# Attention with two heads side by side in the array, and its output projection beside the last batches

## The reference, cut to what matters

```
x = x + tanh(g_xattn[0]) * L0_xattn(layernorm(x), ctx)     # the stage that is changed
x = x + tanh(g_ffn[0])   * L0_experts(layernorm(x))        # 14 routed + 2 shared
x = x + tanh(g_xattn[1]) * L1_xattn(layernorm(x), ctx)
x = x + tanh(g_ffn[1])   * L1_experts(layernorm(x))
def L0_xattn(tgt, src):                                    # 16 heads of 16 features
    q, k, v = tgt @ Wq + bq, src @ Wk + bk, src @ Wv + bv
    w = softmax(q @ k.T / sqrt(16))
    return concat_heads(w @ v) @ Wo + bo
```

## Time and profile before

| what | us |
|---|---|
| median of three runs | 966.05 |
| profiled execution | 963.44 |
| its span, first to last instruction | 961.70 |
| TensorE busy | 754.5 (78%) |
| VectorE busy | 619.2 (64%) |
| ScalarE busy | 481.3 (50%) |
| GpSimd busy | 410.3 (43%) |

### The profile page before, as it was taken

How to read it: one execution, slowest core, us unless ns; L and a number is a source line. 1 busy time by engine, 2 the same in 40 slices (tenths; PEclk the granted TensorE clock), 3 DMA queues, 4 the chain that set the end, 5 groups by cost and what they waited for, 6 DMA issues and landing times. The chain is left out here.

```text
span 961.7 us, 20435 instructions
## 1 busy us (share of the span) xinstructions
PE 754.5 (78%) x6519; PEld 573.3 (60%) x6519; DVE 619.2 (64%) x1458; ACT 481.3 (50%) x989; POOL 410.3 (43%) x437
## 2 busy tenths in 40 slices
PE   4679999999977398979888889578777548998830
PEld 2356667667656398978666656467666526665420
DVE  8567677767664669873444444377788436666766
ACT  4736565556544467652333333245655236776632
POOL 4268323233160028881000000586856716746455
PEclk9779999999999669999999999788989868999985
DMA  6447322223170238753222221378532212323233
GB/s 159 114 103 164 92 61 67 56 64 77 30 243 9 90 88 274 236 186 114 72 66 67 68 70 48 103 192 206 162 107 67 63 53 91 115 72 96 83 90 100
DMA packets 84511, 101.50 MB, mean 106 GB/s; under 512 B 16518, under 2 KB 70758, under 8 KB 84422
## 3 DMA queue, kind: packets, MB, share of 16 engines
q1 hardware_dynamic: 69526, 68.42, 25.4%
q0 software_dynamic: 12960, 30.74, 11.4%
q10 hardware_dynamic: 1936, 1.17, 0.5%
HBM read 61.03 MB, written 24.38 MB: 89 GB/s over the span
## 5 line engine op out<-in xcount | busy, mean ns | idle before, releaser
L645 DVE TENSOR_REDUCE a_mx<-ps 112x2 f32<-112x750 f32 x128 | 119.8, 936 | 45.1 <-PE ps L323 38.7
L529 ACT ACTIVATE a_Pf<-ps 125x672 f32<-125x672 f32 x128 | 89.7, 729 | 15.6 <-PE ps L271 14.6
L323 PE MATMUL ps<-a_stkK,a_stkQ 96*112 96x375 bf16 x256 | 68.2, 349 | 20.8 <-DMA a_stkK<-a_KS 10.6
L51 PE MATMUL ps<-f_w2hi,f_hh 128*128 (+1 forms) x292 | 81.3, 278 | 3.1 <-DVE f_hl L1432 3.1
L1430 DVE CAST f_hh<-ps 128x512 bf16<-128x512 f32 x41 | 28.4, 692 | 83.9 <-PE ps L1171 83.9
L51 PE MATMUL ps<-f_w2lo,f_hh 128*128 (+1 forms) x292 | 81.2, 278 | 0.0
L51 PE MATMUL ps<-f_w2hi,f_hl 128*128 (+1 forms) x292 | 81.1, 278 | 0.0
L51 PE MATMUL ps<-f_w1hi,f_xgThi 128*128 x150 | 57.9, 386 | 23.6 <-DVE f_xgTlo L1423 17.7
L1719 POOL MEMSET a_half<- 112x2 f32 x1 | 0.1, 94 | 170.3 <-POOLq L89 170.3
L546 POOL DMA_DIRECT2D a_stkK<-a_KS x96 | 51.2, 540 | 45.7 <-DVE a_KS L612 28.9
L540 POOL TENSOR_TENSOR a_ctxL<-a_ctxF,a_ctxH 128x750 bf16<-128x750 f32 x16 | 25.7, 1604 | 104.7 <-ACT a_ctxH L429 104.7
(11 more groups left out here) (403 smaller groups left out, 2367.9 us busy)
## 6 DMA issues: line engine op xcount, KB each, us to landing
a_raw<-F_w SPq DMA_DIRECT2D x22, 512.0 KB, 5.9
f_xg<-f_xd SPq DMA_DIRECT2D x75, 128.0 KB, 2.2
f_yd<-f_yo SPq DMA_DIRECT2D x75, 128.0 KB, 1.7
f_raw<-F_w SPq DMA_DIRECT2D x14, 512.0 KB, 4.1
a_ctxF<-ctxT SPq DMA_DIRECT2D x16, 375.0 KB, 3.5
a_cR<-ctx SPq DMA_DIRECT2D x16, 375.0 KB
a_cT_first<-ctxT SPq DMA_DIRECT2D x14, 375.0 KB, 4.9
f_xd<-a_zero POOLq DMA_DIRECT2D x1, 5248.0 KB, 20.0
```

The costliest lines, as they stand in the source:

```text
L51: ins = nc.tensor.matmul(out, l, r, start=first and i == 0, stop=last and i == len(steps) - 1)
L323: last = nc.tensor.matmul(psMX[:T, h, :S], stkQ[0:96, bass.ds(n.b, 1), j // JJ, j % JJ, h * T:(h + 1) * T].rearrange("p o q -> p (o q)"), ...
L529: nc.scalar.activation(Pf[:, s % PB], psST[:C, s % 2, :SC, :QW], ACT.Exp).then_inc(exp_done, 1)
L645: nc.vector.reduce_max(mx[:, n.odd, 2 * j:2 * j + 2], psMX[:T, :, :S], AX).then_inc(mx_red, 1)
```

## The change

- Each head has its own rows. Head h of a pair stands in partitions 64h to 64h + 47 (3 parts of 16 features), with the two rows for the maximum behind them. The queries are not masked; `maxima` contract over 48 rows, twice per step, `scores` over 50 rows, six matmuls of 112 columns per step instead of three of 224. The two heads of a pair write to different PSUM banks. The factor 1/4 moves into the exp.
- Key pieces are 24 a batch instead of 12, of 16 partitions instead of 32 and one run of 750 elements each: 12 from SP and 12 from POOL. SP's are cut in 6 and 6 around `place_maxima`. A placement takes four DMAs instead of two. Keys are made three batches ahead instead of two.
- Query pieces of the first four batches are shared by SP and POOL, the others issued later by ACT and POOL.
- In a step the order on PE is maxima, values, scores, keys, `turn_values`. `values` writes to a free corner of bank 0 (`psPV`), so every second `scores` waits for the copy `oT`. PE's and POOL's lists are written out; SP, ACT and DVE keep their loop over batches 3 to 10.
- `output_projection` is gone as a stage. Its first three groups run in the lists of batches 13, 14 and 15, the last one after them. The zero fill is 14 DMAs of ACT, one a batch, and POOL's bias additions stand in the lists of batches 8 to 11.

```diff
-        stkQ = sb("stkQ", [98, B, KD, JJ, QW], BF16)
-        stkK = sb("stkK", [98, 4, KD, JJ, S], BF16)
+        SIDE, KEYS, DOT = P // 2, 3 * DH, 3 * DH + 2
+        stkQ = sb("stkQ", [P, JJ, B, KD, T], BF16)
+        stkK = sb("stkK", [P, 4, JJ, KD, S], BF16)
...
-        psPV = k.ps[:, 6, 0:T]
+        psPV = k.ps[:, 0, SC * T:(SC + 1) * T]
...
-        PIECES = [(jj, a, part) for a, part in ((0, 0), (1, 1), (2, 0)) for jj in range(JJ)]
+        PIECES = [(jj, h, a, part) for a, part in ((0, 0), (1, 1), (2, 0)) for jj in range(JJ) for h in range(2)]
+        K_SP, K_POOL = PIECES[0::2], PIECES[1::2]
...
                 def place_maxima(n, half):
                     sp.wait_ge(turn_free, 2 * n.b + half + 1)
-                    for part in range(2):
-                        sp.dma_start(stkQ[96 + part:97 + part, bass.ds(n.b, 1), half].rearrange("o b j (h q) -> o (b j h) q", q=T),
-                                     cneg[:, n.odd, half, part, :]).then_inc(c_in[half][n.odd], 16)
+                    for h in range(2):
+                        for part in range(2):
+                            row = SIDE * h + KEYS + part
+                            sp.dma_start(stkQ[row:row + 1, :, bass.ds(n.b, 1), half, :].rearrange("o j b q -> o (j b) q"),
+                                         cneg[JJ * h:JJ * (h + 1), n.odd, half, part, :]).then_inc(c_in[half][n.odd], 16)
...
+                def stack_keys(w, pieces):
+                    at_least(sp, st_full, w.b * NJ - 4 * NJ)
+                    sp.wait_ge(k_free, w.b * KD + KD)
+                    for jj, h, a, part in pieces:
+                        sp.dma_start(stkK[SIDE * h + DH * a:SIDE * h + DH * (a + 1), w.slot, jj],
+                                     KS[2 * DH * jj + DH * h:2 * DH * jj + DH * (h + 1), w.odd, part]).then_inc(k_sp[w.slot], 16)
...
+                    split = 0 if len(ws) == 2 else 6
+                    for w in ws[-1:]:
+                        if split:
+                            stack_keys(w, K_SP[:split])
                     if n is not None:
                         place_maxima(n, 0)
+                    for w in ws[-1:]:
+                        stack_keys(w, K_SP[split:])
...
                     for c in range(SC):
-                        last = nc.tensor.matmul(psST[:C, j % 2, c, :QW],
-                                                stkK[:, b.slot, j // JJ, j % JJ, c * C:(c + 1) * C],
-                                                stkQ[:, bass.ds(b.b, 1), j // JJ, j % JJ, :].rearrange("p o q -> p (o q)"),
-                                                start=True, stop=True)
+                        for h in range(2):
+                            side = slice(SIDE * h, SIDE * h + DOT)
+                            last = nc.tensor.matmul(psST[:C, j % 2, h, c * T:(c + 1) * T],
+                                                    stkK[side, b.slot, j % JJ, j // JJ, c * C:(c + 1) * C],
+                                                    stkQ[side, j % JJ, bass.ds(b.b, 1), j // JJ, :].rearrange("p o q -> p (o q)"),
+                                                    start=True, stop=True)
...
+                for t in range(KD):
+                    turn_rows(LAST, t)
+                for n in range(GB * LAST, B):
+                    project_rows(n)
```

More of the change, by code:

```diff
@@ L205, in run, with task_at, product, maxima_of @@
                 some = lambda r: (at(r),) if at(r) else ()
[L206 to L215, removed]
+                emit(at(-1), at(0), at(1), some(3), some(4), some(5))
+        def task_at(ws, s):
+            if len(ws) == 2:
+                return ws[s // 4], s % 4
+            return (ws[0], s // 2) if ws and s % 2 == 0 else (None, None)
+        def product(w, i):
+            early = isinstance(w.b, int) and w.b in (1, 2) and i % 2 == 1
+            return k.ps[:, 0, :] if early else psP
+        def maxima_of(n, j):
+            early = isinstance(n.b, int) and n.b == 0 and j % 2 == 1
+            return k.ps[:, 2:4, :] if early else psMX
+        def stack_queries(eng, batches, pieces, stacked):
+            for jj, h, i, part in pieces:
+                eng.dma_start(stkQ[SIDE * h + DH * i:SIDE * h + DH * (i + 1), jj, batches],
+                              QS[2 * DH * jj + DH * h:2 * DH * jj + DH * (h + 1), part, batches]).then_inc(stacked, 16)
         with nc.Block() as block:
@@ L235, in emit @@
                         place_maxima(b, 1)
-                    for row in l:
+                    for row in l[0:1]:
                         load(row)
[L238 to L243, removed]
+                    for w in ws[1:]:
+                        stack_keys(ws[0], K_SP)
@@ L363, in _ @@
                 turn_tokens(2)
+                keys(ring(0), 1)
                 queries(1, 0)
@@ L366, in _ @@
                 turn_tokens(3)
-                keys(ring(0), 1)
                 queries(2, 0)
@@ L391, in emit @@
                             turn_maxima(b, 1)
+                        row, g = (p, 3) if s == 1 else (b, s // 2 - 1)
+                        if row is not None and s % 2 == 1:
+                            values(row, g, p.b * NJ + NJ if b is None else b.b * NJ + s)
+                        if b is not None:
+                            scores(b, s)
                         if n is not None and s == 4:
                             turn_maxima(n, 0)
-                        if w is not None and s % 2 == 0:
-                            (keys if s < 4 else vals)(w, s // 2 % 2)
@@ L396, in emit @@
-                        if b is not None:
-                            scores(b, s)
-                        row, g = (p, 3) if s == 1 else (b, s // 2 - 1)
-                        if row is not None and s % 2 == 1:
-                            values(row, g)
-                    if n is not None and isinstance(n.b, int) and n.b == GB - 1:
-                        for g in range(1, NG):
-                            pe.wait_ge(q_in[g], 3 * JJ * 16)
-                run(pe, emit)
+                        w, t = task_at(ws, s)
@@ new lines, in emit @@
+                    if n is not None and n.b in (GB - 1, Q_TURN - 1):
+                        pe.wait_ge(rest_q, 16 * (len(Q_POOL) + (0 if n.b == GB - 1 else len(Q_PIECES))))
+                        pe.wait_ge(act_q, 16 * len(Q_ACT))
+                emit(None, None, ring(0), (ring(1), ring(2)), None, None)
+                for b in range(B + 1):
+                    p, b, n, w = (ring(b + d) if 0 <= b + d < B else None for d in (-1, 0, 1, 3))
+                    emit(p, b, n, (w,) if w else (), None, None)
@@ L632, in _ @@
                 moments(3)
+                low_keys(ring(0), 1)
                 normed(3)
@@ L635, in _ @@
                 queries(1)
-                low_keys(ring(0), 1)
                 x_low(3)
@@ new lines, in emit @@
+                        if b is None and p is not None and s == 1:
+                            for r in range(3):
+                                row_moments(r)
+                run(dve, emit)
+                done = 3
+                for r in range(done, done + 6):
+                    row_moments(r)
+                for t in range(KD):
+                    rows_low(LAST, t)
+                for r in range(done + 6, GB * LAST - 1):
+                    row_moments(r)
+                for r in range(GB * LAST, B):
+                    add_rows(r)
+                    row_moments(r - 1)
@@ L754, in linker @@
+                row_moments(B - 1)
+                for r in range(B):
+                    dve.wait_ge(y_st, r + 1)
+                    nc.vector.bn_aggr(k.mv[:, r, :], stats[:, r, :]).then_inc(y_var, 1)
+                dve.wait_ge(y_var, B)
 def linker(engine, sem):
```

412 lines of the change are left out of this document (216 added, 196 removed).

## The result

The changed kernel takes **974.06 us** (median of 8 runs, 969.97 to 978.97) against 966.27 us (963.08 to 970.23) for the kernel before, run beside it. The ratio is 1.0079, with a 95% interval of 1.0056 to 1.0101. Predicted were 937.5 us with a range of 918 to 956. The forecast was wrong in sign, and so were all rivals with a price but the one that was given 0.05.

What follows compares the result with a forecast made beforehand. TensorE looked like the bound, its steps falling from 15.04 to 13.7 us a batch, with SyncE's chain next at 14.4. The last aggregate at 293.2 instead of 321.76 took 28.6 off 963.44: 934.8, plus 2.6 gives 937.5 us (918 to 956).

Steps and rivals of the forecast that it cites:

- The steps: TensorE and VectorE's eight steps a batch, two heavy: each 0.17 us shorter, 13.7 us a batch instead of 15.04.
- the ring: Light step of TensorE and VectorE around one PSUM pair: 1.64 us before, 1.5 forecast as maxima pairs start together.
- First maxima: Startup: the first maxima matmuls start at about 39 us instead of 45.48.
- SyncE's chain: Closed once a batch: scores, low keys, six pieces, four placements, landing, next scores; forecast 14.4 us (13.6 to 15.3).
- the tail: Batches 13 to 15 and output projection: last aggregate ends at 293.2 us instead of 321.76, including the earlier gains.
- the scores' 48 short matmuls: Scores as 48 matmuls of 112 columns instead of 24 of 224: taken as same cost; half to double possible.
- 11.4 + 6c = 14.4: Sum of the once-a-batch chain through SyncE in us; c = 0.50 is a key piece's 0.45 plus 0.05 between issues.
- scores to low keys: First link of the chain: 6.25 us before, +0.95 for scores ahead of keys, -0.35 for shorter steps, 6.85.
- landing: Last link of the chain: the last placement's landing, about 2.0 us, before the next batch's scores may start.
- dear-piece rival: Key pieces on SyncE at c = 0.65: 15.3 us a batch, only the ends gain, 952.6 us; chance 0.15.
- SyncE becomes the bound outright: Issues dearer, 0.75 a piece and 0.90 a placement: 17 us a batch, 974 us, slower above 16.4; chance 0.05.
- Array switching: TensorE's array drains at some ten more mode switches a batch, 0.18 us each: +1 us a batch, 951; chance 0.10.

Runs made afterwards that it cites:

- share6: Changed kernel with SyncE issuing 6 of a batch's 24 key pieces instead of 12, all behind the first placements, GpSimd 18: 934.71 us, ratio 0.9651.
- order12p2: Changed kernel, pieces still 12 and 12, SyncE's first placements ahead of new pieces and two placements merged into one DMA: 936.84 us, ratio 0.9717.
- place2: Changed kernel with the two halves' placements of the same part merged into one DMA, 4 issues a batch instead of 8: 947.74 us, ratio 0.9798.
- busy20: Changed kernel plus twenty unused matmuls of 176 columns on TensorE ahead of each batch's first scores' wait: 966.37 us, ratio 0.9983.
- split3: Changed kernel with 3 instead of 6 of SyncE's key pieces ahead of the first four placements, 9 behind: 959.68 us, ratio 0.9921.
- split9: Changed kernel with 9 instead of 6 of SyncE's key pieces ahead of the first placements, 3 behind: 1006.59 us, ratio 1.0395.

## Why the prediction was wrong

**Where it was right.** The steps: 13.7 us a batch was forecast for TensorE and VectorE alone, and with the chain out of the way share6 takes 13.79, order12p2 13.74. The maxima's two halves start together, the ring is 1.49 (1.5). First maxima 39.52 (39). Batch 12 to batch 15 in share6 takes 43.12 (41.9 predicted: 14.3 and twice 13.8), batch 15 to the end 24.41 (22.15; 23.34 in the kernel after). TensorE's longest waits are on a_stkQ<-a_cneg at the first scores, at 1.4 to 2.8 us instead of 1. SyncE's chain was named with its right members and called the thing that is late next. Neither the tail nor the scores' 48 short matmuls (six in 0.38, three in 0.45 before) brought a loss.

**The step that failed is the sum of that chain**, 11.4 + 6c = 14.4. By the batch at 230.39 its terms were off by these amounts (measured less predicted):

| term | predicted | measured | off |
|---|---|---|---|
| scores to low keys | 6.85 | 7.96 | +1.11 |
| six pieces | 3.00 | 3.73 | +0.73 |
| gaps | 0.35 | 0.25 | -0.10 |
| placements to the last issue | 2.20 | 2.34 | +0.14 |
| landing | 2.00 | 2.45 | +0.45 |
| sum | 14.40 | 16.73 | +2.33 |

- The price of a piece was taken in the middle of two rows, 0.45. The row on the same two tensors was right and the row of like shape was not; place2 shows why shape is a poor guide, since twice the runs cost nothing. The dear-piece rival covered this, and its 15.3 us a batch would have been 952.6 (its sum comes to 308.6, not 308.3, so 952.9).
- What carried the result beyond that rival was the clock. The chain had no term for what a wait does to the engine that waits. I took 1.00 from the earlier trace rows, a stretch of a kernel that hardly waits, into one that I myself predicted to wait in each batch. busy20 prices it: 1.19 us a batch. The loop feeds itself: the wait lowers the clock, the slower matmuls delay the low keys, these delay the pieces, and the next wait is longer.
- The landing was taken from key pieces as about 2.0, below even the shortest in the row named for it (2.1 to 2.7). It was 2.45 in this batch, and 1.6 to 2.7 over the eleven.
- Single issues of some 1.5 us (L264's longest is 1.698) lengthen some batches further: in the longest, of 18.78, the six pieces took 4.64. They took as long in the shortest, of 15.60, where the clock had held and the landing was 1.64; so these issues alone do not set a batch's length.

**The sums after it.** Batches 1 to 12 took 186.47 us instead of 157.8 (229.1 less 71.3): +28.7. Batch 1 starts at 76.90 instead of 71.3 (+5.6), of which the 30 pieces at 0.12 more make 3.6. Batch 12 to 13 takes 16.14 instead of 14.3 (+1.8), the two after it 28.86 instead of 27.6 (+1.3), the last 23.34 instead of 22.15 (+1.2). With +28.7 these are 38.6, all of the 38.5 us between 293.2 and 331.71.

**The rivals.** "SyncE becomes the bound outright" gave 974 and 17 us a batch with a turning point at 16.4. The numbers came true by luck, its mechanism did not: issues did not get dearer to 0.75 (0.589 in the median, a placement 0.596 and not 0.90), SyncE idles in the batch shown from 235.98, the end of its load, to 238.38, and split3 and split9 show that its sum does not set the time. The turning point was nearly right: with this kernel's own start and end it is (321.76 - 76.90 - 68.34) / 11 = 16.05, where 68.34 is from batch 12's first scores to the last aggregate's end. Array switching: no run shows a loss by it. share6's 13.79 holds the switches as well, and next to the 13.7 forecast without them that leaves little room for the 1 us of that rival. This is argued from a forecast and not shown: no run changed the switches alone.

## What to carry to other kernels

When work on a queue is doubled, write down for each thing on it when its reader needs it, and put what is needed next ahead of what has a batch to spare, above all when a lookahead has just been lengthened. Close each chain that repeats once a period and add it up at the lower clock as well: here a wait of 1.4 to 2.8 us on TensorE in each period cost another 1.2 behind it. For a DMA's issue cost take the row with the same kind of source and destination rather than the one with the same shape, and merge issues before moving them: share6 (6 and 18 pieces) and order12p2 (12 and 12, placements merged) both beat the kernel before by about 3%.

## What the runs showed of the hardware that was not expected

- An SBUF-to-SBUF issue on SyncE took 0.588 to 0.600 us in the median for 16 partitions in one run, 32 in two, 4 runs into one partition, or 8 into two; only the old placement, 8 rows of 112 into one partition, took 0.698. The 0.32 of the earlier trace rows was for a read from DRAM, and the context's load, also from DRAM, took 0.392. What makes the difference was not tried. On GpSimd the piece of 16 partitions took 0.484 to issue, the old one of 32 took 0.536.
- The granted clock did not fall behind every wait. Behind 1.63 us at 198.00 and 1.81 at 163.94 it stayed at 1.00; behind 1.65 at 230.39 it had fallen by 230.91, to the level at which 375 columns take 0.52, and by 235.31 they took 0.33 again. With busy20's waits of up to 0.71 at the first scores the matmuls behind kept 0.32. What decides it, no run here settles.
